# The context of three batches kept as rows of features, with its denominators inverted in 64 columns

## The reference

```
n = layernorm(x);  q, k, v = n @ Wq, n @ Wk, n @ Wv     (16 heads each)
p = softmax over keys of causal(q k^T) / 16
x = x + (p @ v, heads side by side) @ Wo + bo
m = layernorm(x);  m and W rounded to an fp6 grid in blocks of 32, with a scale for each block
x = x + m' @ W'^T + bias
```

## Time and profile before

| | |
|---|---|
| median of 3 runs | 2117.28 us (2115.57 to 2119.65) |
| the profiled execution | 2120.14 us, span 2118.4 us |
| busy: PE, DVE, ACT, POOL | 95%, 82%, 64%, 37% |
| granted PE clock, mean | 0.985 |
| 16 DMA queues, busy | 23.3% |

### The profile page before, as it was taken

One profiled execution on the slowest core, in us unless ns is written; L12 is line 12 of the kernel. 1 busy time (PEld: TensorE's weight loads), 2 busy tenths in 40 slices (PEclk: granted clock), 3 DMA queues, 4 the chain that ended last, 5 costly groups with the idle time before them and its releaser, 6 DMA issues.

```text
span 2118.4 us, 36179 instructions
## 1 busy us (share of the span) xinstructions
PE 2012.2 (95%) x12037; PEld 792.0 (37%) x12037; DVE 1739.8 (82%) x4442; ACT 1365.3 (64%) x2905; POOL 783.3 (37%) x1099
## 2 busy tenths in 40 slices
PE   6799899999999999999999999999999999999994
PEld 3333333333333444343333344434333343333433
DVE  4797897878988787888888788796898998888875
ACT  5357666766766666667665666676666666777661
POOL 3323324231435454543324556363143443111232
PEclk9899999999999999999999999999999999999997
DMA  4441221313040322312122231221403112030000
GB/s 153 128 103 54 59 74 37 94 46 97 19 101 26 97 64 72 101 42 87 49 62 58 79 87 63 66 87 49 118 4 101 42 44 57 25 92 24 9 31 20
DMA packets 178327, 138.72 MB, mean 65 GB/s; under 512 B 54486, under 2 KB 178140, under 8 KB 178140
## 3 DMA queue, kind: packets, MB, share of 16 engines
q1 hardware_dynamic: 178140, 136.40, 23.3%
HBM read 85.20 MB, written 50.33 MB: 64 GB/s over the span
## 4 chain that ended last, share of the span: by engine, by line
PE 72%; DVE 16%; ACT 3%; issue 3%; SPq 2%; POOL 2%; DMA 2%; POOLq 0%; DVEq 0%; ACTq 0%
PE psum L1397 21%; PE psum L1380 19%; PE psum L1365 16%; PE psum L1463 7%; DVE max_parts L1108 7%; PE psum L1456 5%; DVE psum L1103 3%; ACT probs L911 2%; PE psum L1432 1%; SPq L633 1%; PE psum L1415 1%; ACT acc_sb L918 1%; PE psum L1485 1%; DMA out_shop<-ctx_scratch 1%; DVE max_parts L1103 1%
## 5 line engine op out<-in xcount | busy, mean ns | idle before, releaser
L911 ACT ACTIVATE probs<-psum 128x512 f32<-128x512 f32 (+3 forms) x2560 | 1213.3, 537 | 527.4 <-PE psum L1380 521.8
L1108 DVE TENSOR_REDUCE max_parts<-psum 128x1 f32<-128x512 f32 x1536 | 968.3, 683 | 130.0 <-PE psum L1365 125.6
L1380 PE MATMUL psum<-q_rows,k_rows 99*128 99x512 bf16 (+3 forms) x2560 | 857.4, 351 | 3.4 <-ACT probs L911 1.6
L1365 PE MATMUL psum<-k_rows,q_rows 96*128 96x512 bf16 (+3 forms) x2560 | 816.6, 350 | 25.8 <-DVE max_parts L1108 10.2
L1397 PE MATMUL psum<-probs,v_in 128*17 128x512 f32 (+3 forms) x5120 | 595.4, 537 | 10.6 <-ACT acc_sb L918 9.9
L1103 DVE CUSTOM_DVE_ANT_0 psum<-psum,causal 128x128 f32<-128x128 f32 (+3 forms) x1024 | 475.9, 519 | 133.4 <-PE psum L1365 130.2
L1380 PEld LDWEIGHTS psum<-q_rows,k_rows 99*128 99x128 bf16 x2560 | 237.2, 97 | 632.0 <-ACT probs L911 496.3
L748 POOL TENSOR_SCALAR_AFFINE_SELECT probs<-probs 128x512 f32<-128x512 f32 x256 | 165.2, 645 | 788.7 <-ACT probs L911 788.3
L1365 PEld LDWEIGHTS psum<-k_rows,q_rows 96*128 96x128 bf16 x2560 | 245.1, 98 | 277.8 <-DVE max_parts L1108 65.3
L1397 PEld LDWEIGHTS psum<-probs,v_in 128*17 128x17 f32 x5120 | 85.8, 95 | 226.9 <-issue 165.0
L1103 DVE DVE_READ_ACCUMULATOR2_ANT max_parts<- 128x1 f32 x1024 | 145.0, 142 | 0.0
(11 more groups left out here) (158 smaller groups left out, 1374.7 us busy)
## 6 DMA issues: line engine op xcount, KB each, us to landing
q_rows<-qk_scratch SPq DMA_DIRECT2D x384, 64.0 KB, 2.6
k_rows<-qk_scratch SPq DMA_DIRECT2D x384, 64.0 KB, 2.7
qk_scratch<-shop SPq DMA_DIRECT2D x56, 384.0 KB, 2.9
shop<-in_L_attn_x SPq DMA_DIRECT2D x19, 512.0 KB, 4.0
v_scratch<-shop SPq DMA_DIRECT2D x16, 544.0 KB, 4.0
v_in<-v_scratch SPq DMA_DIRECT2D x64, 136.0 KB, 2.6
ctx_scratch<-ctx_out SPq DMA_DIRECT2D x60, 128.0 KB, 1.7
out_shop<-in_L_attn_x SPq DMA_DIRECT2D x12, 512.0 KB, 5.4
```

The source lines that it names most:

```text
L911: nc.scalar.activation(probs[s % NPROBS][:, h, a:CHUNK], bank[SCORE_BANKS[n % 3]][:, a:CHUNK], ACT.Exp, scale=SCALE).then_inc(probs_ready, 1)
L1108: nc.vector.tensor_reduce(max_parts[k % 2][:, first:first + heads, t % TILES, c], ring_bank(UNIT_USE[n])[:, 0:heads * width] .rearrange("p ...
L1365: ins = nc.tensor.matmul(dst[:, i * width:(i + 1) * width], q_rows[u][0:ROWS, qc, first + i, t % TILES * P:(t % TILES + 1) * P], k_rows[u] ...
L1380: nc.tensor.matmul(bank[SCORE_BANKS[n % 3]][:, a:CHUNK], k_rows[u][0:ROWS + LEVELS, h, kb * P:(kb + 1) * P], q_rows[u][0:ROWS + LEVELS, qc ...
```

## The change

For the first 48 `k` (three batches: `by_rows`) the bank copied by ACT goes to memory as it is, 128x512 floats (256 KB), without being turned or divided. When the fourth head group of a chunk is stored, SP loads its 16 rows of 512 denominators as 128x64, DVE inverts them, SP stores them and loads them again with each row repeated on 16 partitions, into `outT`. The sums are loaded as rows of features (two DMAs), POOL multiplies the two in halves (`weigh`), and `attend` reads the product. `turn_acc`, `normalise`, `turn_ctx` and ACT's copy of it are left out for these batches. `acc_sb` has two buffers. The last batch works as before.

The diff, without the pieces that only pass arguments or create semaphores:

```diff
@@ -225,6 +225,12 @@
+def by_rows(k):
+    return k < NK - QC * QC
...
@@ -241,7 +247,7 @@
-    p = by_items(p, 0.45, "turn_ctx")
+    p = by_items(p, 0.45, "turn_ctx") if quick else by_pool(p, 1.3, "weigh")
     p = by_items(p + 1 + (p < TAIL), 1.95, "attend")
...
@@ -304,10 +310,21 @@
     done_at = FIRSTS[k] + SIZES[k] + 1
+    if by_rows(k):
+        STORED[k] = p = done_at + 1
+        sync(p, "store_ctx", k)
+        if k // QC % QC == QC - 1:
+            n = k // (QC * QC) * QC + k % QC
+            sync(p + 2, "load_den", n)
+            p = vector(p + 5, 0.6, "invert", n) + 1
+            sync(p, "store_inverse", n)
+            INVERTED[n] = p
+        continue
     TURNED[k] = item(done_at + 1, 0.45, "turn_acc", k)
     spend("vector", TURNED[k] + 1, 0.7)
     if k < NK - QC:
-        sync(TURNED[k] + 2, "store_ctx", k)
+        STORED[k] = TURNED[k] + 2
+        sync(STORED[k], "store_ctx", k)
...
@@ -328,16 +345,17 @@
         if late(n):
-            load = max(TURNED[k - QC] + 4, NS - GROUP_STEPS + 2 if before is None else READ_AT[before] + 2)
+            load = max(STORED[k - QC] + 2, NS - GROUP_STEPS + 2 if before is None else READ_AT[before] + 2)
             ready = max(TURNED[k] + 1, load + 2)
         else:
-            load = max(TURNED[k] + 4, free)
-            ready = load + 2
+            load = max(INVERTED[n] + 2, free)
+            sync(load, "load_inverse", n)
+            ready = load + 5
         sync(load, "load_ctx", n)
         sync(max(load, free), "load_again", n)
         ready = max(ready, free)
         ends = [place_output(n, a, ready) for a in range(2)]
-        READ_AT[n], DONE_AT[n] = STAGE["turn_ctx"], ends[-1]
+        READ_AT[n], DONE_AT[n] = STAGE["turn_ctx" if late(n) else "attend"], ends[-1]
 for g in range(NG):
...
@@ -389,14 +407,20 @@
-def ctx_groups(n):
-    return H // HG - late(n)
+def ctx_loads(n):
+    return H // HG - 1 if late(n) else 2 * EH
+def ctx_loaded_by(n):
+    return 16 * sum(ctx_loads(m) for m in range(n + 1) if out_set(m) == out_set(n))
 def layer_kernel(nc, x, wq, wk, wv, wo, bo, wf, bf, out):
     qk_scratch = nc.dram_tensor("qk_scratch", [2, LEVELS, E, B * C], BF16, kind="Internal").ap()
     v_scratch = nc.dram_tensor("v_scratch", [B, QC, H // HG, P, TILES * HG * VW], F32, kind="Internal").ap()
+    sums_scratch = nc.dram_tensor("sums_scratch", [B, QC, H // HG, P, CHUNK], F32, kind="Internal").ap()
+    inverse_scratch = nc.dram_tensor("inverse_scratch", [B, QC, H, CHUNK], F32, kind="Internal").ap()
     ctx_scratch = nc.dram_tensor("ctx_scratch", [B, QC, H // HG, P, TILES * HG * D], F32, kind="Internal").ap()
...
@@ -651,6 +692,11 @@
                 g, qc = divmod(k, QC)
+                if by_rows(k):
+                    sp.wait_ge(acc_copied, k + 1)
+                    sp.dma_start(sums_scratch[g // QC, qc, g % QC], acc_sb[k % 2][:, :]
+                                 ).then_inc(ctx_stored[k % 2], 16)
+                    return
                 sp.wait_ge(vector_emptied, ITEM_NO["turn_acc", k])
...
@@ -673,10 +719,43 @@
                         sp.wait_ge(v_stored[u], 16 * NCH // 2)
-                for g in range(ctx_groups(n)):
-                    sp.dma_start(ctx_in[w][:, :, g * HG * D:(g + 1) * HG * D],
-                                 ctx_scratch[b, c, g].rearrange("p (j n) -> p j n", j=TILES)
+                if late(n):
+                    for g in range(H // HG - 1):
+                        sp.dma_start(ctx_in[w][:, :, g * HG * D:(g + 1) * HG * D],
+                                     ctx_scratch[b, c, g].rearrange("p (j n) -> p j n", j=TILES)
+                                     ).then_inc(ctx_loaded[w], 16)
+                    return
+                rows = sums_scratch[b, c].rearrange("g (h r) n -> (g h) r n", r=32)
+                for e in range(EH):
+                    sp.dma_start(ctx_rows[w][:, e, :], rows[e * H // EH:(e + 1) * H // EH, 0:D, :]
                                  ).then_inc(ctx_loaded[w], 16)
+            def load_den(n):
+                b, c = divmod(n, QC)
+                k = (QC * (b + 1) - 1) * QC + c
+                sp.wait_ge(ctx_stored[k % 2], 16 * (k // 2 + 1))
+                wait(sp, inverse_stored, 16 * n)
+                sp.dma_start(den[:, :], sums_scratch[b, c].rearrange("g (h r) (s n) -> (g h) r s n", r=32, s=P // H)
+                             [:, D, :, :]).then_inc(den_loaded, 16)
+            def store_inverse(n):
+                b, c = divmod(n, QC)
+                sp.wait_ge(dens_inverted, n + 1)
+                sp.dma_start(inverse_scratch[b, c].rearrange("h (s n) -> (h s) n", s=P // H), den[:, :]
+                             ).then_inc(inverse_stored, 16)
+            def load_inverse(n):
+                w = out_set(n)
+                b, c = divmod(n, QC)
+                before, times = before_in_set(n)
+                sp.wait_ge(inverse_stored, 16 * (n + 1))
+                if before is not None:
+                    sp.wait_ge(for_vector, ITEM_NO["feed", before, 1])
+                for e in range(EH):
+                    sp.dma_start(outT[w][:, e, :], inverse_scratch[b, c][e * H // EH:(e + 1) * H // EH, None, :]
+                                 .broadcast_to([H // EH, D, CHUNK])).then_inc(ctx_loaded[w], 16)
...
@@ -789,6 +874,13 @@
+            def weigh(n, a):
+                w = out_set(n)
+                pool.wait_ge(ctx_loaded[w], ctx_loaded_by(n))
+                mine = half_tokens(ctx_rows[w], a)
+                nc.gpsimd.tensor_tensor(out=mine, in0=mine, in1=half_tokens(outT[w], a), op=ALU.mult
+                                        ).then_inc(ctx_weighed, 1)
...
@@ -913,9 +1007,11 @@
                 act.wait_ge(values_done, FIRSTS[k] + SIZES[k])
-                if k:
-                    act.wait_ge(for_vector, ITEM_NO["turn_acc", k - 1])
-                nc.scalar.copy(acc_sb[:, :], acc_bank).then_inc(acc_copied, 1)
+                if k >= 2 and by_rows(k - 2):
+                    act.wait_ge(ctx_stored[k % 2], 16 * (k // 2))
+                elif k >= 2:
+                    act.wait_ge(for_vector, ITEM_NO["turn_acc", k - 2])
+                nc.scalar.copy(acc_sb[k % 2][:, :], acc_bank).then_inc(acc_copied, 1)
...
@@ -1120,7 +1213,7 @@
                 nc.vector.reciprocal(inv_den[:, :, :], turned[:, :, :, D]).then_inc(den_inverted, 1)
-                dve.wait_ge(den_inverted, k + 1)
+                dve.wait_ge(den_inverted, k - (NK - QC * QC) + 1)
                 if k < NK - QC:
...
@@ -1185,6 +1278,10 @@
+            def invert(n):
+                dve.wait_ge(den_loaded, 16 * (n + 1))
+                nc.vector.reciprocal(den[:, :], den[:, :]).then_inc(dens_inverted, 1)
...
@@ -1435,10 +1534,8 @@
                 w = out_set(n)
-                loads = sum(ctx_groups(m) for m in range(n + 1) if out_set(m) == w)
-                pe.wait_ge(ctx_loaded[w], 16 * loads)
-                if late(n):
-                    pe.wait_ge(vector_emptied, ITEM_NO["turn_acc", NK - NCH + n])
+                pe.wait_ge(ctx_loaded[w], ctx_loaded_by(n))
+                pe.wait_ge(vector_emptied, ITEM_NO["turn_acc", NK - NCH + n])
                 turn_half(ITEM_USE["turn_ctx", n, a], ctx_in[w], a)
...
@@ -1486,13 +1583,17 @@
             def attend(n, a):
-                pe.wait_ge(scalar_emptied, ITEM_NO["turn_ctx", n, a])
+                if late(n):
+                    pe.wait_ge(scalar_emptied, ITEM_NO["turn_ctx", n, a])
+                else:
+                    pe.wait_ge(ctx_weighed, 2 * n + a + 1)
                 pe.wait_ge(later_loaded, N_LATER)
                 pe.wait_ge(bias_ready, 2)
                 use = ITEM_USE["attend", n, a]
                 emptied(pe, use)
                 bias(use, 0)
-                linear(use, (2 * a, 2 * a + 1), outT[out_set(n)], w_o, False).then_inc(for_vector, 1)
+                linear(use, (2 * a, 2 * a + 1), (outT if late(n) else ctx_rows)[out_set(n)], w_o, False
+                       ).then_inc(for_vector, 1)
```

More of the change, by code:

```diff
@@ L434, in layer_kernel @@
         probs = [sbuf(f"probs{u}", [HG, CHUNK]) for u in range(NPROBS)]
-        acc_sb = sbuf("acc_sb", [CHUNK])
+        acc_sb = [sbuf(f"acc_sb{u}", [CHUNK]) for u in range(2)]
+        den = sbuf("den", [H * CHUNK // P])
         max_parts = [sbuf(f"max_parts{u}", [HG, TILES, QC]) for u in range(2)]
@@ L482, in layer_kernel @@
             list(buffers) for buffers in zip(*(output_buffers(place) for place in places)))
+        ctx_rows = [t.rearrange("p (e n) -> p e n", e=EH) for t in ctx_in]
         for w in range(NSETS):
@@ L545, in layer_kernel @@
         x_again = [sem(f"x_again{w}") for w in range(NSETS)]
+        den_loaded = sem("den_loaded")
+        dens_inverted = sem("dens_inverted")
+        inverse_stored = sem("inverse_stored")
+        ctx_weighed = sem("ctx_weighed")
         moments2_ready = sem("moments2_ready")
@@ L582, in emptied, with half_tokens, ctx_read @@
                     eng.wait_ge(vector_emptied, count)
```

(25 more changed lines are left out.)

6 lines of the change are left out of this document (2 added, 4 removed).

## The result

The median is 2090.45 us in 4 runs (2085.36 to 2093.93), against 2116.81 us before in 4 runs; the recorded ratio is 0.9861 with a 95% interval of 0.9846 to 0.9876. Of 2117 us that is 29.4 us less (26.2 to 32.6). The two medians are 26.4 us apart, a ratio of 0.9875, near the upper end of that interval. The profiled execution took 2085.36 us, at the fast end of its runs.

The account below looks back on a forecast made before the run. PE was taken to set the pace, with DVE not far behind. Gains of 34.8 us less costs of 1.2, 1 and 1 made 31.6 us off 2120.1: 2088.5 us, forecast as a 2086 us median, range 2068 to 2106.

Parts of the forecast that it names:

- the two stretches: Distance between the same points of two batches, 503.84 us for 160 slots, forecast to fall by 10 to 11 us.
- rival A: DVE takes the time freed on PE and output work is packed anew; half the gains left, 14 us, 2103 us; chance 0.17.
- Who sets a slot: PE's 205 waits for DVE's banks in 640 steps: DVE paces 0.32 of the slots, PE 0.68.
- `turn_acc` and `normalise`: Removed 48 times each, 0.44 us of PE and 0.67 us of DVE, weighted by who paces: 24.7 us gained.
- turn_ctx: 24 halves removed, 0.44 us of PE each, gained only where PE paces (0.68): 7.2 us.
- The wait for the context: PE stood still three times for the context load; its 2.9 us in all counted as gained.
- Rival B: More gained: normalise and turn_ctx in full, late-load bubble of the order of 13 us; 2067 us after costs; chance 0.12.
- The inversion: Added 12 times on DVE, taken as 0.30 us each, 0.32 of it on the path: 1.2 us cost.
- Its wait: DVE stops until denominators land; 0 to 1.5 us at 3 of 12 chunks, behind twelve load_rows DMAs: 1 us cost.
- POOL's product: weigh, 24 times on POOL at 1.25 us, mostly hidden between masks: 1 us cost, 6.7 if each delayed a mask.
- The lock on the shared ports: POOL's product may block DVE's instructions with two SBUF inputs; counted as nothing, bounds 0 to 25 us of DVE.
- The packing of the slots: Output work placed anew in the slots; mentioned only within rival A, with no size of its own.

Follow-up runs that it names:

- b_all1: Kernel before with a quarter of turn_acc and normalise for 48 k, and turn_ctx of 12 chunks replaced by one bf16 matmul of zeros; 0.9935, 13.8 us faster.
- b_ready5: Kernel before with turn_ctx five slots behind the load of the context instead of two, nothing left out; 0.9977, 4.9 us faster.
- a_kept_room33: Kernel after with the removed work's room kept free and projections 33 slots apart instead of 30; 0.9875, 3 us slower than the kernel after.
- a_ready3: Kernel after with POOL's product three slots behind SP's load instead of five; 0.9937, 16 us slower than the kernel after.
- a_ready9: Kernel after with POOL's product nine slots behind SP's load instead of five; 0.9915, 11 us slower than the kernel after.
- a_kept_room: Kernel after with the planner keeping the slot room of turn_acc and normalise free, same work; 2077.92 us, 0.9801, 12.7 us faster than the kernel after.
- b_turn1: Kernel before with one transpose instead of four in turn_acc for the first 48 k; 0.9969, 6.6 us faster.
- b_both1: Kernel before with one transpose in turn_acc and normalise on one tile of four for the first 48 k; 0.9949, 10.8 us faster.
- b_norm2: Kernel before with DVE's product of normalise done twice for the first 48 k; 1.0041, 8.7 us slower.
- a_invert4: Kernel after with DVE's inversion on 4 of 64 columns; 0.9852, 1.9 us faster than the kernel after.

## Why the prediction was right

Forecast were 31.6 us less, measured 29.4 us (26.2 to 32.6; 26.4 by the medians), and 11.1 and 12.4 us in the two stretches, where 10 to 11 us were said. The mechanism held in kind: PE and DVE both set the time, and both lose work. Its sizes held less well, and a part of the agreement is luck. One sign of rival A was seen as well: PE's waits for DVE's banks grew, from 86.3 to 109.8 us, but the distance between batches fell by 11 to 12 us, not by A's 5 or less.

- **Who sets a slot.** Taken as 0.68 PE and 0.32 DVE from the count of waits. For PE that was too much: by changed loads its work counts for 0.42 (0.28 to 0.56), or 0.50 in the stretch of the middle. DVE's counts for 0.47 when added (0.31 to 0.63) and 0.37 when removed, but for 0.30 and 0.29 in that stretch, so whether 0.32 was too little is open. For `turn_acc` and `normalise` this hardly changes the sum, since both were removed from the same `k`: 21.1 us x 0.42 + 32.3 us x 0.42 = 22.4 us instead of 24.7.
- **turn_ctx.** Taken as 7.2 us. Its 10.6 us of PE at 0.42 would be 4.4 us; b_all1, which takes away half of them, leaves it open.
- **The wait for the context.** Taken as 2.9 us; b_ready5 gave 4.9 (2.5 to 7.2), packing included. Rival B's 13 us for it are out. B's own terms, 32 + 10.6 + 13 less the costs, add up to 52 us, not the 50 written there.
- **The inversion** was mis-sized: 0.547 us instead of 0.30, 12 x 0.547 x 0.42 = 2.8 us instead of 1.2. Its length goes by the columns (see the last section), so neither the reciprocal of 16 columns nor a product of 256 in 0.425 us could stand for 64.
- **Its wait** was 0.2 us in all, less than the 1 us counted, but the reasoning was too sure: one landing took 8.2 us, and a_kept_room33 shows the stop behind the twelve DMAs, 2.99 us at the place named, the first chunk of a batch, and 6.35 and 6.78 us at a second chunk, where none was expected.
- **POOL's product** was counted at 1 us, with 6.7 as bound: nothing measurable. Its cover of 15.7 us was nearly enough, with 7.5 us of waiting in five cases, though the loads of x took 8.5 us and not 5.4; with two slots less it costs 16 us (a_ready3). DVE's busy time fell by 23.2 us and POOL's rose by 27.4, where 28 and 30 were said.
- **The lock on the shared ports.** The Trainium skill, SBUF — State Buffer, section "Who interferes with whom", lets a POOL product hold back a DVE instruction with two SBUF inputs. Making POOL's new product small left DVE's such instruction at a mean of 782 ns against 783, with the same long ones (1.75 us the longest) in both, so for this change the rule priced nothing. (The prediction has "once 1.748"; in the kernel before 3 of the 24 took over 1 us, 1.10, 1.10 and 1.75.) Whether another of POOL's instructions holds those long ones back no run here tested.
- **The packing of the slots** is the term that the sum did not have; it stood only as half a sentence in rival A. Four slots more between load and use cost 11 us (a_ready9), two lines of the planner gave 12.7 us (a_kept_room), both with unchanged work. With the terms as measured the sum is 22.4 + 4.4 + 4.9 - 2.8 = 28.9 us beside 29.4, closer than the terms' own intervals allow one to claim. It is also closer than it should be: b_turn1, b_both1 and b_norm2 leave every slot in its place, so their shares speak for a kernel whose freed room stays empty, and that one, a_kept_room, gained 42 us. The 13 us between are in no term: either a microsecond is worth more when all of the work goes than when a part of it does, or the other places of the output work gave them. No run separates the two. So the forecast came out with two things against each other: its terms gave too little for the work removed, and the filled room, which it did not count, took back 12.7 us.

## What to carry to other kernels

- Where two engines both stand near the limit, change the load of each by a known amount, down and up, and read what comes through. A count of waits told who waits, but it gave 0.68 where a microsecond of PE was worth 0.42. Such a share holds for the plan in which it was taken: with slots placed anew it missed by 13 us.
- When work is removed from a planned order, leave the holes open first, and let the planner fill them only as a second, separate step. Here the two lines that did so were worth 12.7 us; a shift of other work by three slots on top lost them again.
- A queue that issues in order delays what stands behind a burst: a small load with a waiter on the critical engine should have its place ahead of the burst. That is a suggestion from a_kept_room33; no run here tried it.

## What was not expected of the hardware

- Of the loads of the denominators (32 KB, median 2.2 us to landing in the kernel after) one took 8.2 us, and one in a_kept_room33 10.5 us.
- A reciprocal costs DVE about 6 to 7 ns for each further column, wherever its source lies: 128x4 took 174 ns in SBUF (a_invert4) and 173 ns from PSUM (b_both1), 128x16 253 and 248 ns, and 128x64 in SBUF 547 ns.
